# A graph attention layer on one core: the second phase over a ring of three K|V groups, with V scaled one group late

## The reference, cut to what matters

```python
L, C, H, E = (4096, 512, 8, 131072); D = C // H; HID = 1024     # all float32
z = _ln(x, ln1_g, ln1_b)
q, k, v = (z @ Wq + bq), (z @ Wk + bk), (z @ Wv + bv)           # each [L, H, D]
scores = einsum('ehd,ehd->eh', q[row], k[col]) * scale + bias   # row = src, col = dst, E edges
p = exp(scores - segment_max(scores, row)[row])
alpha = p / segment_sum(p, row)[row]
att = segment_sum(alpha[:, :, None] * v[col], row).reshape(L, C) @ Wo + bo
x1 = x + att
z = _ln(x1, ln2_g, ln2_b)
y = x1 + silu(z @ W1 + b1) @ W2 + b2
return _layernorm(x + y)
```

## Time and profile before

| what | us |
|---|---|
| median of three runs | 4619.97 |
| those runs | 4613.76, 4619.97, 4627.66 |
| span of the profiled execution | 4610.2 |
| busy in it: TensorE, VectorE, ScalarE, GpSimd | 3227.0, 2862.0, 2094.3, 3100.7 |

### The profile page before, as it was taken

The page is one execution under the profiler, slowest core; times in us unless marked ns, Lnnn a source line. Parts: engine busy times, 40 slices in busy tenths (PEclk is TensorE's granted clock), DMA queues, the critical chain, the costliest instruction groups (busy, mean ns, idle before and its releaser), DMA issues.

```text
span 4610.2 us, 73226 instructions
## 1 busy us (share of the span) xinstructions
PE 3227.0 (70%) x18717; PEld 2461.0 (53%) x18717; DVE 2862.0 (62%) x6445; ACT 2094.3 (45%) x6748; POOL 3100.7 (67%) x3033
## 2 busy tenths in 40 slices
PE   4576877776877546777677776777777777777766
PEld 3344444444444235666565665656656555656655
DVE  9766666666666335666556665666565565665654
ACT  0011112111111135666566666666566566665664
POOL 0177777777777767777777777777676676666752
PEclk5577766777767668888888888888888888888888
DMA  4233333333334355655666656665665665656542
GB/s 168 66 113 115 107 102 112 109 102 107 112 100 111 102 192 188 208 183 184 222 203 214 214 196 205 221 214 182 213 210 166 210 206 190 203 185 211 189 150 82
DMA packets 282999, 756.58 MB, mean 164 GB/s; under 512 B 92435, under 2 KB 94675, under 8 KB 281862
## 3 DMA queue, kind: packets, MB, share of 16 engines
q0 software_dynamic: 213664, 577.32, 38.1%
q1 hardware_dynamic: 68454, 169.70, 12.1%
HBM read 759.20 MB, written 58.87 MB: 177 GB/s over the span
## 4 chain that ended last, share of the span: by engine, by line
issue 23%; PE 21%; POOL 16%; DVE 14%; DMA 11%; DVEq 9%; ACT 3%; POOLq 1%; ACTq 1%; SPq 0%; PEld 0%; PEldq 0%
POOL records L378 8%; PE bank L1144 7%; DMA records<-rec_w,pos_i 5%; PE bank L1179 5%; POOL region_a L447 5%; DVE region_c L864 4%; PE bank L1227 3%; DMA region_a<-kv,cols 3%; DVEq L990 2%; DMA region_c<-hiT 2%; PE bank L1201 2%; DVEq L792 2%; DVE hi_oh L728 2%; ACT region_a L669 1%; PE bank L1093 1%
## 5 line engine op out<-in xcount | busy, mean ns | idle before, releaser
L447 POOL DMA_INDIRECT region_a<-kv,cols x1160 | 1311.3, 1130 | 449.5 <-issue 342.5
L378 POOL DMA_INDIRECT records<-rec_w,pos_i x1024 | 1046.9, 1022 | 534.3 <-issue 515.1
L669 ACT ACTIVATE region_a<-region_a,pr 128x64 f32<-128x64 f32 x4640 | 1132.5, 338 | 58.5 <-issue 46.6
L1179 PE MATMUL bank<-ident,region_a 128*128 128x128 f32 x4640 | 708.2, 308 | 345.5 <-issue 281.8
L864 DVE TENSOR_TENSOR region_c<-region_a,region_c 128x1024 f32<-128x1024 f32 x580 | 734.4, 1308 | 283.8 <-DMA region_a<-kv,cols 239.4
L1144 PE MATMUL bank<-ident,region_c 128*128 128x128 f32 x4640 | 664.9, 307 | 329.2 <-DVE region_c L864 329.0
L1179 PEld LDWEIGHTS bank<-ident,region_a 128*128 128x128 f32 x4640 | 619.1, 161 | 425.0 <-issue 322.6
L1144 PEld LDWEIGHTS bank<-ident,region_c 128*128 128x128 f32 x4640 | 624.1, 201 | 373.0 <-DVE region_c L864 372.9
L1093 PE MATMUL bank<-region_c 64*128 64x64 f32 x2048 | 346.4, 337 | 204.7 <-issue 178.9
L1093 PEld LDWEIGHTS bank<-region_c 64*128 64x128 f32 x2048 | 327.7, 248 | 293.4 <-issue 259.4
L542 ACT COPY rec_w<-region_a 128x64 f32 x128 | 31.3, 245 | 960.5 <-DMA records<-rec_w,pos_i 960.5
(11 more groups left out here) (147 smaller groups left out, 4264.8 us busy)
## 6 DMA issues: line engine op xcount, KB each, us to landing
region_c<-srcT SPq DMA_DIRECT2D x128, 512.0 KB
region_c<-hiT SPq DMA_DIRECT2D x128, 256.0 KB
region_a<-kv,cols POOLq DMA_INDIRECT x1160, 5.8
records<-rec_w,pos_i POOLq DMA_INDIRECT x1024
kv<-region_c SPq DMA_DIRECT2D x32, 512.0 KB
records<-pad_rec SPq DMA_DIRECT2D x16, 576.0 KB, 16.9
region_a<-in_x_dram SPq DMA_DIRECT2D x32, 256.0 KB
qx<-region_a SPq DMA_DIRECT2D x32, 256.0 KB
```

The lines of the kernel that those rows point to most:

```text
L378: pool.indirect_dma_start(records, bass.IndirectOffsetOnAxis(ap=pos_i[j % 2][:, s:s + 1], axis=0), rec_w[j % 2][:, s, :], None).then_inc(S ...
L447: pool.indirect_dma_start(KV[h][:, s, :], None, kv, bass.IndirectOffsetOnAxis(ap=cols[h][:, s:s + 1].bitcast(I32), axis=0), bounds_check=L ...
L669: last = act.activation(v, v, ACT.Copy, scale=pr[h][:, s, hd:hd + 1])
L1179: last = pe.matmul(vT_ps[:, c * P:(c + 1) * P], KV[h][:, s, C + c * P:C + (c + 1) * P], ident[:, :], start=s == 0 and c == 0, stop=s == GR ...
```

## The change

**Ring.** `region_a` holds three groups (RING) in place of two, for which some arrays of the first phase move between regions. The code of each engine stands three times, and `by_ring` picks the slot. GpSimd now holds for the sums of three groups ago.

**Records by tile.** Rows start at multiples of five blocks in the table, so one indirect DMA fetches all records of a tile's first five blocks (`load_tile`), one tile ahead, in stage 2; q comes with it into one of two buffers. The row numbers are loaded by the sync queue two tiles ahead. The table has 40960 blocks in place of 24576 and is cleared by 32 writes of 480 KB in place of 16 of 576 KB. The copies of biases, columns, row numbers and q are gone: the engines read the records where they landed. A sixth or later block is loaded in `late_records`, as it is needed, and waited for.

**V one group late.** Slots 0 to 3 are scaled by ScalarE, slots 4 to 7 by VectorE, and VectorE's `weigh` of a group stands behind the products of the next one. TensorE sums all four pairs of the group before in the body of the next; VectorE adds up a group's sum two bodies later (`collect`). The softmax takes the running maximum as a ninth entry of one reduction and one subtraction.

**Tails.** The dense part is shifted by about a stage, as the code shows. Both bias adds move from GpSimd to VectorE in the first phase, which writes x + bo and x + b2 to a DRAM table (`x_rows`); GpSimd fetches these rows in stage 1 (`load_x`). The inverse square roots are worked out on VectorE with integer and multiply steps (`inverse_roots`), and ScalarE's table for the exponent is loaded once ahead of the phase. The weights of the dense part load after the ranking instead of beside it, and TensorE waits for them at its first projection only.

The core of the diff, with added and kept lines only (what is removed stands in the kernel above):

```diff
+RING = 3
...
+        def tile_groups(eng, n, first, body, alone, reset=None, enter=None):
+            for g in range(2):
+                body((first + g) % RING, g)
...
             with eng.If(n > PEEL):
+                if enter:
+                    enter((first + PEEL - 1) % RING)
+                with eng.Fori(0, (n - (PEEL - RING + 1)) // RING) as i:
                     if reset:
                         reset()
+                    body((first + PEEL) % RING, PEEL)
+                    for more in range(1, RING):
+                        with eng.If(n > i * RING + (PEEL + more)):
+                            body((first + PEEL + more) % RING, PEEL)
+                    eng.nop()
...
+            with sp.Fori(0, NT // 2 - 1) as i:
+                for u in range(2):
+                    sp.wait_ge(S["rec_loaded"], i * 32 + (u + 1) * 16)
+                    sp.wait_ge(S["q_loaded"], i * 32 + (u + 1) * 16)
+                    sp.wait_ge(S["xb_loaded"], i * 32 + (u + 1) * 16)
+                    sp.dma_start(row_w[u][:, :], rows_ranked[bass.ds(i * (2 * P) + (2 + u) * P, P), :]).then_inc(ROW_LOADED[u], 16)
...
+            def load_tile(u):
+                pool.indirect_dma_start(rec_tile[:, u * FRONT:(u + 1) * FRONT, :].rearrange("p s r -> p (s r)"), None, areas,
+                                        bass.IndirectOffsetOnAxis(ap=row_w[u][:, 1:2].bitcast(I32), axis=0)).then_inc(S["rec_loaded"], 16)
+                pool.indirect_dma_start(row_q[:, u * C:(u + 1) * C], None, q_rows, row_number(u)).then_inc(S["q_loaded"], 16)
+            def load_x(u):
+                pool.indirect_dma_start(x_w, None, x_rows, row_number(u)).then_inc(S["xb_loaded"], 16)
...
+            def gather(r, of):
                 g = pool.snap(groups)
+                for s in range(GROUP):
+                    if s % 2 == 0:
+                        hold(S["summed"], g * PAIRS + s // 2 + 1)
+                    pool.indirect_dma_start(KV[r][:, s, :], None, kv,
+                                            bass.IndirectOffsetOnAxis(ap=of[:, s, HEADS:HEADS + 1].bitcast(I32), axis=0),
+                                            bounds_check=L - 1, oob_is_err=False).then_inc(KVS[r][s // 2], 16)
+                pool.reg_add(groups, groups, 1)
+                if r == 0:
+                    pool.reg_add(since, since, 1)
...
+            def late_records(r, u):
+                hold(S["summed"], pool.snap(groups) * PAIRS + 1)
+                pool.tensor_scalar(idx[r][:, :], idx[(r + RING - 1) % RING][:, :], 1.0, row_w[u][:, 2:3], ALU.add, ALU.min).then_inc(S["idx_set"], 1)
                 pool.reg_add(n_idx, n_idx, 1)
...
+                    n = pool.snap(count, min_val=2, max_val=NBLK)
+                    def alone(stage):
+                        if stage == 1:
+                            next_count(pool, t, count)
+                            with pool.If(t > 0):
+                                hold(S["s_ready"], t)
+                                load_x(1 - u)
+                        if stage == 2:
+                            with pool.If(t > 2):
+                                pool.reg_add(n_sent, n_sent, 1)
+                                hold(S["out_ready"], pool.snap(n_sent))
+                                send()
+                            with pool.If(t < NT - 1):
+                                hold(ROW_LOADED[1 - u], i * 16 + (u + 1) * 16)
+                                hold(S["q_loaded"], t * 16 + 16)
+                                hold(S["sc_ready"], pool.snap(before))
+                                load_tile(1 - u)
+                    def body(r, stage):
+                        if stage == 0:
+                            pool.reg_mov(before, groups)
+                            hold(S["rec_loaded"], t * 16 + 16)
+                        if stage < PEEL:
+                            at = u * FRONT + stage * GROUP
+                            gather(r, rec_tile[:, at:at + GROUP, :])
+                        else:
+                            late_records(r, u)
+                            gather(r, rec_late[r])
+                        alone(stage)
+                    def enter(r):
+                        pool.tensor_scalar(idx[r][:, :], row_w[u][:, 1:2].bitcast(I32), float(PEEL), float(PEEL - 1),
+                                           ALU.mult, ALU.add).then_inc(S["idx_set"], 1)
+                        pool.reg_add(n_idx, n_idx, 1)
+                        hold(S["idx_set"], pool.snap(n_idx))
...
+            act.preload_act_table(ACT.Exp)
...
+                def body(r, stage):
                     g = act.snap(groups)
                     take_scT()
                     if stage == 0:
                         with act.If(t > 0):
                             take_vT()
                     else:
                         take_vT()
+                    act.wait_ge(S["sc_ready"], g + 1)
+                    act.activation(pr[r][:, 0:GROUP + 1, :], sc[r][:, :, :], ACT.Exp).then_inc(S["p_ready"], 1)
                     act.drain()
+                    weigh(r)
                     act.reg_add(groups, groups, 1)
+                    alone(stage)
...
+                dve.bn_aggr(mv[:, 0:2], stats[:, :]).then_inc(S["stats1"], 1)
+                dve.wait_ge(S["x_out"], it * 16)
+                dve.tensor_tensor(xb_row[:, 0:C], x_in, bo_all, ALU.add)
+                dve.tensor_tensor(xb_row[:, C:2 * C], x_in, b2_all, ALU.add).then_inc(S["xb_ready"], 1)
...
+            def weigh(r):
+                dve.wait_ge(S["p_ready"], dve.snap(groups))
+                for s in range(SUB, GROUP, 2):
+                    v = KV[r][:, s:s + 2, C:2 * C].rearrange("p s (h d) -> p s h d", h=HEADS)
+                    dve.tensor_tensor(v, v, pr[r][:, s + 1:s + 3, :].unsqueeze(3).broadcast_to([P, 2, HEADS, D]),
+                                      ALU.mult).then_inc(S["v_dve"], 1)
...
+            def collect(r):
+                add_sum()
+                scale(r, acc)
+                add_weights(r)
+                dve.drain()
...
+            def softmax(r, bias, fresh):
+                m_new = sc[(r + 1) % RING][:, 0, :]
+                if fresh:
+                    dve.memset(sc[r][:, 0, :], FLOOR)
+                dve.wait_ge(S["sc_summed"], dve.snap(groups) + 1)
+                dve.tensor_tensor(sc[r][:, 1:GROUP + 1, :], sc_ps.rearrange("p (s h) -> p s h", s=GROUP), bias, ALU.add)
+                dve.drain()
+                dve.tensor_reduce(m_new, sc[r][:, :, :].rearrange("p s h -> p h s"), AX.X, ALU.max)
+                dve.drain()
+                dve.tensor_tensor(sc[r][:, :, :], sc[r][:, :, :], m_new.unsqueeze(1).broadcast_to([P, GROUP + 1, HEADS]),
+                                  ALU.subtract).then_inc(S["sc_ready"], 1)
+                dve.drain()
...
+                dve.tensor_scalar(var_w[:, :], mv[:, :].rearrange("p (a b) -> p b a", b=2)[:, 1, :], EPS, None, ALU.add)
+                dve.drain()
+                dve.tensor_scalar(root[:, :].bitcast(I32), var_w[:, :].bitcast(I32), -0.5, SEED, ALU.mult, ALU.add)
+                for three in (3.0, 12.0, 768.0):
+                    dve.drain()
+                    dve.tensor_tensor(root_t[:, :], root[:, :], root[:, :], ALU.mult)
+                    dve.drain()
+                    dve.tensor_tensor(root_t[:, :], root_t[:, :], var_w[:, :], ALU.mult)
+                    dve.drain()
+                    dve.scalar_tensor_tensor(root[:, :], root_t[:, :], -three, root[:, :], ALU.add, ALU.mult)
+                dve.drain()
+                dve.tensor_scalar(rstd[:, :], root[:, :], 2.0 ** -13, None, ALU.mult)
+                dve.drain()
+            def middle(k):
...
+                dve.wait_ge(S["xb_loaded"], k * 16)
+                dve.wait_ge(S["wo_done"], k)
+                dve.tensor_tensor(z2, wo_ps[:, :], x_w[:, 0:C], ALU.add)
+                dve.drain()
+                dve.bn_stats(stats[:, :], z2)
+                dve.drain()
+                dve.bn_aggr(mv[:, 0:2], stats[:, :])
+                dve.drain()
+                inverse_roots()
+                dve.tensor_scalar(z2n, z2, mv[:, 0:1], rstd[:, 0:1], ALU.subtract, ALU.mult).then_inc(S["z2_ready"], 1)
...
                 def gap(stage):
+                    if stage == 0:
+                        with dve.If(t > 1):
+                            dve.reg_add(older, older, 1)
+                            silu(dve.snap(older), 0)
+                    if stage == 1:
+                        with dve.If(t > 1):
+                            silu(dve.snap(older), 1)
+                    if stage == 2:
+                        with dve.If(t > 1):
+                            last_stats(dve.snap(older))
                     if stage == 3:
                         next_count(dve, t, count)
                         with dve.If(t > 0):
+                            middle(t)
                     if stage == 4:
                         with dve.If(t > 1):
```

(66 more changed lines are left out.)

709 lines of the change are left out of this document (273 added, 436 removed).

## The result

Before 4617.4 us (4 runs), after 4666.2 (4 runs): 1.010 times as long, 95% interval 1.008 to 1.013. The forecast was 4085. The profiled execution spans 4664.5 us, its granted clock 0.796.

A forecast was written before the change was run, and what follows sets the result against it. Bound by the order in which engines wait for each other. Second phase 986 + 1250 + 115 less 27: 2324 us for 2864.0; 4610.2 - 540 + 5 = 4075 profiled, 4085 median; range 3900 to 4290.

The forecast's parts named there:

- Stage 4 to the next 0 ... 13.9: From a five-group tile's last group to the next tile's first: 11.9 plus ScalarE's half hidden layer, 2.0, makes 13.9 us.
- the 22.1: From a four-group tile's last group to the next tile's first, the last two stages standing behind each other: 22.1 us.
- the wait for K and V: VectorE's wait in the second phase: 1.56 us a group kept for tiles of five and more, 0.78 for the others.
- stage 0 to 1: A tile's first group to its second: TensorE's half of up and down, scores, fold and V sums take 16.2 us.
- stage 1 to 2: A tile's second group to its third, the plain cycle: 11.9 us.
- The signs named beforehand: Wrong if intervals inside tiles stay above 16.5 us, the K and V wait exceeds 3 a group, or gathers pass 1.5.
- What the prediction said would be seen: 14 to 17 us within tiles, 22 to 23 after four-group tiles, DMA 0.75 to 0.8, TensorE near 0.85 busy.
- The boundary is long because nothing of a new tile is fetched before its row numbers, its records and its q have come: Kernel before, between tiles: these fetches come one after another, making the boundary 31.7 us against 16.6 inside tiles.
- GpSimd as the bound: Rival, chance 0.05: every gather blocked as the longest was, 21.0 us a group on GpSimd, 4780 us in all.
- The cycle of a group: Second phase: chain from ScalarE's exponent through V scaling, fold and V sums to the next exponent, 11.9 us.
- no late transfers: Rival, chance 0.14: the ring hides all waits for K and V, 175 us less than the sum: 3910 us.
- The clock: TensorE's stages use the full level; a fall would double 2.3 us, at most 2.3 a group; nothing taken.

The follow-up runs named there:

- straight after: The changed kernel with group counts written in, its second phase straight-line code on all engines (also called the straight-line version): 4012.3 us, 0.867 of the kernel before.
- With the read moved: The changed kernel in straight-line code, with VectorE's read of the next tile's group count in stage 0 instead of stage 3: 3958.1 us, 0.857.

## Why the prediction was wrong

- **What failed is the step "Stage 4 to the next 0 ... 13.9", and with it the 22.1.** The step lists engines' work and nothing of the sequencer: that the code stands in three copies, and that every boundary leaves one, was in the diff and was priced at nothing. The run without jumps has 13.4 where the forecast had 13.9. With jumps it is 35.7 after five groups and 44.1 after four. The 654 us of control flow are more than the whole miss of 581: straight after is 4012, inside the range of 3900 to 4290. That it lies so near 4085 is partly luck. The sum had 175 us too much for the wait for K and V and about 40 in stage 0 to 1, and about 100 too little for the read of the count and 50 in stage 1 to 2.
- **The signs named beforehand didn't catch it.** The intervals inside tiles are 14.6 and not over 16.5, the wait for K and V is far under 3 us a group, a gather 1.246 us, under 1.5. None of the three looks at the boundary. What the prediction said would be seen does show the miss: 44.1 us after a tile of four for 22 to 23, a DMA share of 0.60 for 0.75 to 0.8, TensorE 0.66 busy for 0.85.
- **The kernel before.** "The boundary is long because nothing of a new tile is fetched before its row numbers, its records and its q have come": right in kind, far too large in size. At the boundaries VectorE waited for K and V 3.2 us of 31.6, and 7.2 of 27.0 once the jumps were gone. The reading "inside a tile VectorE waits 223.2 us in all" was wrong too: 98.8 of them lie in the boundaries. The change took this wait away (at no boundary after does VectorE wait for K and V) and put a longer one in its place; none of my rivals was of this kind. The slower one, GpSimd as the bound, didn't happen: a gather took 1.246 us at the mean (0.992 at the median, 2.040 at most) where 1.17 was foreseen, and GpSimd's busy time fell from 1997 to 1558.
- **The cycle of a group** was right where it could be seen. With the read moved the stages are 16.0, 13.6, 12.4, 17.0 and boundaries of 13.4 and 23.0, against 16.2, 11.9, 12.4, 16.9, 13.9 and 22.1. Only stage 1 to 2 was undersized, by 1.7.
- **A term left out:** VectorE's read of the count, 2.6 us in stage 3 to 4 and 3.9 in the four-group boundary.
- **The wait for K and V** of 1.56 or 0.78 us a group was hardly there: 20.5 us in all after the change. In the straight-line version the phase has a DMA share of 0.76, close to the 0.78 forecast, and the wait is still only 24.6. The rival "no late transfers" was right in this. What hides them is the ring of three: with two the wait is 828.5.
- **The clock** took nothing in the straight-line version, as booked: 0.91 in its second phase. In the kernel after it is 0.82, since TensorE stands still at the boundaries, and it adds the 1.8 us a boundary told above.
- **ScalarE's table loads** went, as said: 258 in the second phase before, none after.
- **The start**, +5, measured +5.2 (first softmax at 1675.6 against 1670.3). The end behind the last softmax was booked at 0 and took 9.7 more (85.6 against 75.9); why wasn't tried.

The sum after: inside -229, boundaries +268, start +5, end +10: +54 us, the distance of the two profiled executions (4664.5 and 4610.2).

## What to carry to other kernels

Count the taken branches between the last work of one iteration and the first of the next, on each engine, and how much code each passes over: here a far one costs 3 to 8 us, a near one 0.14, and dead code counts like any other. A buffer ring chosen by a static index multiplies the loop body; lay its copies in the order in which they are used, so that one falls into the next, before judging what the ring is worth. In a profile the sign is "issue" of several us in the chain of waits with all engines idle.

## What the runs showed of the hardware

- One far jump, over 600 drains, idled VectorE 4.1 us (47.9 to 178.0 us over 32). The 94 jumps over copies of the tile code took it 3.3 to 7.6 us each, 5.5 at the mean, and 4.5 where no other engine jumped. What else makes them differ (distance, place in the code) stays open.
- Near jumps took 0.14 us and cost nothing that a run could tell (0.914 to 0.917 of before with, 0.915 without).
- Reading one count from DRAM into a register of VectorE took 5.2 us in one tile; of the 63 loads of its reads the shortest took 0.71 us and the longest 4.73.
- The instruction queues' bytes are no measure of this: their share is 1.3% in all, and the boundaries they belong to are 27% of the span (31 x 40.3 of 4664.5).
